# The clipping and scaling steps of a 4-bit quantiser on GpSimd in place of VectorE

## The reference, cut to what matters

```python
xh = x @ H
scale = clip(max(abs(xh), axis=-1), 1e-05) / 7
xq = clip(round(xh / scale), -8, 7) * scale
ffn = einsum('bsi,oi->bso', xq, wq)          # wq: ternary(weight) * scale
x = x + tanh(g_ffn[0]) * ffn                 # x enters the rotation through a layer norm
```

## Time and profile before

| | |
|---|---|
| median of 3 runs | 267.69 us (267.55 to 268.81) |
| the profiled execution | 269.31 us, of which the span from the first to the last instruction is 267.3 us |
| granted TensorE clock, mean over the span | 0.998 |
| instructions | 6698: PE 1899, PEld 1899, DVE 654, ACT 451, POOL 272 |
| DMA | 31.86 MB moved, mean 119 GB/s |

### The profile page before, as it was taken

The page is one execution under the profiler, slowest core; times in us unless marked ns, Lnnn a source line. Parts: engine busy times, 40 slices in busy tenths (PEclk is TensorE's granted clock), DMA queues, the critical chain, the costliest instruction groups (busy, mean ns, idle before and its releaser), DMA issues. The chain is left out here.

```text
span 267.3 us, 6698 instructions
## 1 busy us (share of the span) xinstructions
PE 252.2 (94%) x1899; PEld 198.7 (74%) x1899; DVE 210.1 (79%) x654; ACT 188.5 (71%) x451; POOL 181.7 (68%) x272
## 2 busy tenths in 40 slices
PE   7997999999788999999999999999999999999894
PEld 4664667777557777778777888777787778999893
DVE  3899899999999896799667877777798625995573
ACT  2488889998799777857776867677788564544562
POOL 5667999985889665745844575449758795954380
PEclk9999999999999999999999999999999999999999
DMA  6458352300025854645584766756552051212530
GB/s 204 154 156 284 143 194 85 120 0 4 1 46 117 183 111 101 142 94 121 124 214 119 185 174 177 195 134 174 131 139 52 17 147 39 78 43 81 165 98 20
DMA packets 25475, 31.86 MB, mean 119 GB/s; under 512 B 4000, under 2 KB 18144, under 8 KB 25312
## 3 DMA queue, kind: packets, MB, share of 16 engines
q1 hardware_dynamic: 25008, 31.23, 43.3%
q10 hardware_dynamic: 432, 0.22, 0.3%
HBM read 14.32 MB, written 2.42 MB: 63 GB/s over the span
## 5 line engine op out<-in xcount | busy, mean ns | idle before, releaser
L637 POOL TENSOR_SCALAR probs<-probs,rsum 128x512 f32<-128x512 f32 x128 | 88.3, 696 | 49.9 <-DVE rsum L996 49.1
L783 ACT ACTIVATE probs<-masked,neg_max 128x512 f32<-128x512 f32 x128 | 91.7, 718 | 11.8 <-DVE neg_max L987 8.8
L1320 PE MATMUL bank<-ident,probs 128*128 128x128 f32 x512 | 78.5, 276 | 2.6 <-DVE probsT L1004 1.2
L1320 PEld LDWEIGHTS bank<-ident,probs 128*128 128x128 f32 x512 | 58.7, 141 | 19.2 <-issue 10.3
L987 DVE CUSTOM_DVE_ANT_0 masked<-bank,mask 128x512 f32<-128x512 f32 x64 | 43.8, 684 | 15.2 <-PE bank L1456 14.6
L792 ACT ACTIVATE probsT<-bank 128x512 f32<-128x512 f32 x74 | 43.6, 589 | 15.1 <-PE bank L1320 14.7
L1493 PE MATMUL bank<-probsT,val 128*32 128x256 f32 (+1 forms) x512 | 46.6, 384 | 0.0
L1004 DVE COPY probsT<-bank 128x512 f32<-128x512 f32 x54 | 36.7, 680 | 8.8 <-PE bank L1320 8.6
L987 DVE CUSTOM_DVE_ANT_0 masked<-bank,shared 128x512 f32<-128x512 f32 x64 | 43.3, 677 | 0.1
L1493 PEld LDWEIGHTS bank<-probsT,val 128*32 128x32 f32 (+1 forms) x512 | 24.4, 123 | 18.0 <-issue 4.8
L1449 PE MATMUL bank<-parts 128*128 128x512 f32 x64 | 31.1, 486 | 1.6 <-DVE neg_max L987 1.3
(11 more groups left out here) (254 smaller groups left out, 517.8 us busy)
## 6 DMA issues: line engine op xcount, KB each, us to landing
k_both<-k_low SPq DMA_DIRECT2D x32, 128.0 KB, 3.0
k_both<-k_high SPq DMA_DIRECT2D x32, 128.0 KB, 2.8
q<-q_split SPq DMA_DIRECT2D x32, 128.0 KB, 2.4
probsT<-staged_gate SPq DMA_DIRECT2D x32, 128.0 KB, 3.0
q<-q_split SPq DMA_DIRECT2D x32, 64.0 KB, 2.1
parts<-staged_k SPq DMA_DIRECT2D x7, 256.0 KB, 2.7
w_flat<-in_w SPq DMA_DIRECT2D x1, 1536.0 KB, 7.2
staged_q<-q_split SPq DMA_DIRECT2D x4, 256.0 KB, 2.6
```

The source lines that it names most:

```text
L637: pool.tensor_scalar(p, p, rsum[:, u % NCOL:u % NCOL + 1], 1.0, ALU.mult, ALU.mult).then_inc(normed, 1)
L783: act.activation(probs[:, u % NP, :], masked[:, u % NS, :], ACT.Exp, scale=-1.0, bias=neg_max[:, c:c + 1], accum_out=sums[:, c:c + 1]).the ...
L1320: ins = pe.transpose(dst[0:rows, t * P:t * P + P], src, ident[:, :])
```

## The change

Three steps leave VectorE's `quantise`: the upper bound with the subtraction of the rounding constant over both tiles, and the lower bound with the scale for each tile. The same three are now a function `clip` of GpSimd, called in its iteration `Y_DONE[0, b] + 5` (42 and 74), behind the `norm`, the split and what else that iteration has, for each batch. The function waits for `job_free` of `rotate`, which VectorE raises with its second rounding step, and between its first and its other steps for its own semaphore `clipped`. It raises `xq_ready` as VectorE did. VectorE no longer waits for its own rounding.

```diff
+        clipped = sem("clipped")
...
+            def clip(b):
+
+                pool.wait_ge(*freed(("rotate", b)))
+                pool.tensor_scalar(tmp[:, :, :], tmp[:, :, :], 1.5 * 2.0 ** 23 + 7.0, -1.5 * 2.0 ** 23, ALU.min, ALU.add).then_inc(clipped, 1)
+                pool.wait_ge(clipped, b + 1)
+                for t in range(NQ):
+                    pool.tensor_scalar(xq[:, t, :], tmp[:, t, :], -8.0, qs[:, 1, t:t + 1], ALU.max, ALU.mult).then_inc(xq_ready, 1)
...
                     if t == Y_DONE[0, b] + 1:
                         rstd_of(1, b)
+                    if t == Y_DONE[0, b] + 5:
+                        clip(b)
                     if t == Y_DONE[0, b] + 11:
                         rows_of(2, b)
...
                     dve.tensor_scalar(tmp[:, t, :], raw[:, t, :], qs[:, 2, t:t + 1], rounder, ALU.mult, ALU.add).then_inc(job_free[i], 1)
-                    dve.wait_ge(*freed(j))
-                    step(dve.tensor_scalar(tmp[:, :, :], tmp[:, :, :], rounder + 7.0, -rounder, ALU.min, ALU.add))
-                    for t in range(NQ):
-                        dve.tensor_scalar(xq[:, t, :], tmp[:, t, :], -8.0, qs[:, 1, t:t + 1], ALU.max, ALU.mult).then_inc(xq_ready, 1)
```

## The result

The changed kernel takes 272.03 us (median, 271.68 to 273.41) against 268.04 for the kernel before (267.55 to 268.81): a ratio of 1.015, with a 95% interval of 1.0128 to 1.0171. It is **slower by 4.0 us**; forecast were 268.3 us and a range up to 270.2. The profiled execution took 272.18 us with a span of 270.3. Ratios compare executions in the same state; one of before_xq_one_later, 348.74 us at a mean granted clock of 0.659, is left out of its ratio.

A forecast was written before the change was run, and what follows sets the result against it. The prediction took TensorE as the bound from 100 us on, and before that a round in which VectorE, ScalarE and TensorE wait by turns. Batch 0's +0.6 us on the 267.69 median, batch 1 nothing, gave 268.3 us; range 267.4 to 270.2.

The forecast's parts named there:

- Where it is paid: Batch 0's turn_xq, where in-order TensorE waits: +0.6 us kept to the end; batch 1 costs and gains nothing.
- The sum: Main case, chance 0.43: batch 0 costs +0.6 us, batch 1 nothing, giving 268.3 us.
- Batch 1's cover: Batch 1's clip ends at 121.65, turn_xq runs at 123.53: 1.9 us early, so the addition costs nothing.
- The price of the three steps: Clip on GpSimd: 0.404 + 2 x 0.376 = 1.16 us, plus 0.08 for the wait between.
- The high end: Clip on GpSimd at 2.9 us, if L627's price comes from a slower path that min and max take too.
- the low row: GpSimd price of 0.376 us for 128x128 with one per-partition scalar, taken for each L1102 step.
- rival 2: min and max slow on GpSimd, 2.9 us in place of 1.16: +2.3 us, 270.0; chance 0.18.
- What a stall of 3.3 us costs at full clock: TensorE standing 3.3 us, not 1.25, before batch 0's turn_xq: +0.6 us reaches the end.
- rival 1: TensorE loses its clock in batch 0's long stall, adding 1.1 us: +1.7 in all, 269.4; chance 0.20.
- rival 4: VectorE is the bound after all, batch 1's 1.46 us come through: -1.4 us, 266.3; chance 0.04.
- the two slow rivals: TensorE's clock loss (chance 0.20) and slow min and max (0.18); both together were placed outside the range.
- Rival 3: Batch 0's lateness is absorbed by idle time before 100 us: 0 to +0.2 us, 267.8; chance 0.15.

The follow-up runs named there:

- before_xq_one_later: Kernel before, quantiser on VectorE, with turn_xq and ffn each one iteration later in the hand-written order, both batches: 1.0006 of the kernel before.
- prices: Kernel before with 22 GpSimd instructions added at the program's end, 11 forms of tensor_scalar at 128 and 256 columns: 279.8 us, one execution.
- warm: Changed kernel with 18 useless matmuls on TensorE ahead of batch 0's wait for xq_ready: 270.27 us, 1.0066 of the kernel before.
- fast_warm: Changed kernel with multiply for min and max (bounds left out) and 10 matmuls in the stall: 268.35 us, 1.0024 of the kernel before.
- b0_only: Changed kernel with the three steps on GpSimd for batch 0 alone, batch 1 on VectorE: 272.88 us, 1.0154 of the kernel before.
- fast_forms: Changed kernel with multiply in place of min and max on GpSimd, bounds left out: 269.34 us, 1.0043 of the kernel before.
- b1_only: Changed kernel with the three steps on GpSimd for batch 1 alone, batch 0 on VectorE: 268.32 us, 1.0011 of the kernel before.

## Why the prediction was wrong, point by point

- **Where it is paid: right.** Batch 0 alone, by TensorE in order behind `turn_xq`, with the delay carried to the end; batch 1 nothing (1.0011). The sum had TensorE without a gap from 100 us on; it has two waits, 0.23 at 118.00 and 0.37 at 119.10, but the changed kernel has the same two, so they took up nothing. Batch 1's cover shrank to 0.43 us, where the sum had 1.9. The copy of unit 44 and the copy `xqT` are the two things that end the lead of their engines, as the sum said.
- **The price of the three steps: the step that failed.** "I take 0.404 + 2 x 0.376 = 1.16" measured 1.09 + 1.54, with a gap of 0.11 between them 2.74 us, so TensorE stood 4.72 us and not 3.3. The high end, 2.9, was built from L627's row and was nearly the truth. I chose the low row by the count of per-partition scalars; the prices run shows that the operation decides, and L627's subtract was the only `tensor_scalar` row on GpSimd outside mult and add. It deserved the larger chance (rival 2 had 0.18). Rival 2's price for it, +2.3, was near what warm measures for the long stall at full clock: +1.92 on the ruler, +1.95 by the medians.
- **What a stall of 3.3 us costs at full clock: right in kind.** Forecast +0.6, measured +0.40 on the ruler (fast_warm). Counted from the last score, the copy of unit 44 came 0.37 us later (forecast 0.5) and the copy `xqT` 0.63 later (0.75).
- **The clock: the second step that failed.** The sum had no term for it; it was left to rival 1, at a chance of 0.20, with 1.1 us as its price. It happened: 1.42 us on the ruler in the changed kernel, about 2.7 in b0_only's profiled execution (17.96 less warm's 15.22), 1.43 in fast_forms. By medians it is 272.03 against 270.27. The price was too low because the work doubled nearly whole, not by 40% (start of a turn to the next score 0.72 for 0.36, `turn_xq` to `ffn` 3.02 for 1.62), because all of that reached the path and not two thirds, and because some executions had the low level for longer. The Trainium skill, TensorE: Matmul & The Clock Gate, section Why this matters for your kernels, warns of idle gaps between bursts; the trace agrees (granted clock 0.66 over 70:74 behind a gap of 4.72 us), and it deserved more weight than "TensorE was busy right up to 67.10".
- **Two rivals taken as alternatives.** By its own sizes the text would have given 0.6 + 1.7 + 1.1 = +3.4 us for both together, 271.1, and the measurement is +4.0. But it said "outside it lie rival 4 and the two slow rivals together". They aren't independent: the slow forms lengthen the very stall in which the clock falls. With the stall of 4.7 us all ten executions had a mean of 0.994 or less, where 57 of the kernel before had 0.997 or more.
- **Rivals 3 and 4.** Rival 3 (absorbed) is true of 1.46 of the first 1.86 us of delay; rival 4 (VectorE the bound) finds nothing in b1_only.

## What to carry to other kernels

Before an elementwise step moves to another engine, look for that engine's price of the same operation, not of the same shape: the rows of GpSimd had 0.40 for 256 columns, and min took 1.07. Where an in-order TensorE waits for the moved step, ask how long the whole gap becomes: a little of it is covered by what the others do in advance, the rest is paid one for one, and a gap that lets the clock fall is paid a second time. Matmuls with no use in such a gap show in one run how much of the loss is clock.

## What the runs showed of the hardware that had not been expected

- GpSimd's `tensor_scalar` has two classes of speed on float32: 0.84 ns a column for mult and add, 3.2 to 3.3 for min, max and subtract (128 and 256 columns, constants). The Trainium skill, GPSIMD Engine Reference, section Engine selection, calls one-input operations roughly line-rate; the runs agree for mult and add alone, and for min, max and subtract the measurement decides: 1.07 us for 256 columns against VectorE's 0.30.
- The share that the clock takes differs between executions of one kernel: 271.4 to 273.0 us for b0_only, in step with the mean granted clock (0.991 to 0.987). In its profiled execution the granted clock is 0.50 from 71 to 77, in the changed kernel's only over 72:74, behind stalls of 4.71 and 4.72 us.
